# Moving the V projection's PSUM evictions from VectorE to ScalarE in an eight-core latent-attention layer

## The reference

```python
q_c = hidden_size @ Wq_c.T + bq_c
q = (q_c @ Wq_up.T + bq_up).reshape(b, s, NH, Q_HEAD).transpose(0, 2, 1, 3)
kv = hidden_size @ Wkv_c.T + bkv_c
kv_nope, kv_rope = (kv[..., :KV_LORA], kv[..., KV_LORA:])
kvu = (kv_nope @ Wkv_up.T + bkv_up).reshape(b, s, NH, QK_NOPE + V_HEAD).transpose(0, 2, 1, 3)
k_nope, v = (kvu[..., :QK_NOPE], kvu[..., QK_NOPE:])
k = jnp.concatenate([k_nope, broadcast(kv_rope)], axis=-1)
attn = softmax(q @ k.T / np.sqrt(Q_HEAD))
out = einsum('bhsv,Hv->bsH', attn @ v, Wo) + bo
```

## Time and profile before

| | us |
|---|---|
| two timed runs | 8833.02, 9584.68 (median 9208.85) |
| the profiled execution | 8920.18, span of its slowest core (core 1) 8918.6 |
| shortest span of a core in it | 8794.0 (core 6) |

### The profile page before, as it was taken

How to read it: one execution, slowest core, us unless ns; L and a number is a source line. 1 busy time by engine, 2 the same in 40 slices (tenths; PEclk the granted TensorE clock), 3 DMA queues, 4 the chain that set the end, 5 groups by cost and what they waited for, 6 DMA issues and landing times.

```text
span 8918.6 us, 102703 instructions; the slowest of 8 cores (8794.0 to 8918.6 us)
## 1 busy us (share of the span) xinstructions
PE 6759.7 (76%) x29896; PEld 2578.0 (29%) x29896; DVE 3238.8 (36%) x5966; ACT 3435.4 (39%) x5611; POOL 90.2 (1%) x168
## 2 busy tenths in 40 slices
PE   3555554555458898899889889889889889854878
PEld 1222222222223323323323322332332332312333
DVE  1112222222225534544543553553553553534111
ACT  2112333333314455355346346337337336442000
POOL 0000000000000000000000000000000000000000
PEclk9777676676679999999999999999999999966777
DMA  5552121111130000000000000000000000023343
GB/s 114 111 100 85 62 79 66 68 69 72 72 89 11 23 15 9 23 15 9 23 15 9 23 16 7 23 16 7 23 23 5 19 23 8 1 81 113 80 109 85
DMA packets 84513, 400.50 MB, mean 45 GB/s; under 512 B 7843, under 2 KB 20260, under 8 KB 65316
## 3 DMA queue, kind: packets, MB, share of 16 engines
q1 hardware_dynamic: 56678, 274.91, 8.6%
q0 software_dynamic: 27328, 119.02, 7.5%
HBM read 466.78 MB, written 46.14 MB: 58 GB/s over the span
## 4 chain that ended last, share of the span: by engine, by line
PE 68%; DVE 13%; issue 9%; DMA 8%; ACT 1%; another core or an unknown queue 1%; DVEq 0%; SPq 0%; ACTq 0%; POOL 0%; POOLq 0%
PE ps L692 8%; PE ps L316 7%; PE ps L656 7%; PE ps L978 6%; PE ps L650 6%; PE ps L706 6%; PE ps L695 5%; PE ps L653 5%; PE ps L370 5%; PE ps L573 4%; PE ps L538 3%; DVE arena L613 3%; DMA arena<-wqcT 2%; DVE arena L272 2%; DMA arena<-x_rot 2%
## 5 line engine op out<-in xcount | busy, mean ns | idle before, releaser
L667 ACT ACTIVATE arena<-ps,sb_negc_col 128x512 bf16<-128x512 f32 x2048 | 1407.9, 687 | 2542.5 <-DVE sb_negc_col L639 1647.1
L678 DVE TENSOR_TENSOR arena<-arena 128x512 bf16<-128x512 bf16 x2048 | 867.1, 424 | 2439.1 <-ACT arena L667 2282.8
L669 ACT ACTIVATE arena<-ps,sb_negc_col 128x512 bf16<-128x512 f32 x2048 | 1394.2, 681 | 0.0
L370 PE MATMUL ps<-sb_id,arena 128*128 128x128 f32 x2048 | 611.8, 348 | 984.8 <-DVE arena L272 955.4
L316 PE MATMUL ps<-arena 128*128 128x512 bf16 (+1 forms) x2560 | 813.3, 425 | 51.2 <-issue 51.2
L692 PE MATMUL ps<-arena 128*128 128x512 bf16 x2048 | 811.5, 396 | 38.7 <-DVE arena L743 38.0
L650 PE MATMUL ps<-arena 128*128 128x512 bf16 x2048 | 807.5, 394 | 31.5 <-ACT arena L669 31.5
L660 PE MATMUL ps<-arena 64*128 64x512 bf16 x2048 | 811.3, 396 | 0.0
L656 PE MATMUL ps<-arena 64*128 64x512 bf16 x2048 | 811.1, 396 | 0.0
L653 PE MATMUL ps<-arena 128*128 128x512 bf16 x2048 | 799.0, 390 | 0.0
L695 PE MATMUL ps<-arena 128*128 128x512 bf16 x2048 | 789.7, 386 | 0.0
(11 more groups left out here) (91 smaller groups left out, 4981.1 us busy)
## 6 DMA issues: line engine op xcount, KB each, us to landing
arena<-x_rot SPq DMA_DIRECT2D x72, 2048.0 KB, 7.8
arena<-wqcT POOLq DMA_DIRECT2D x64, 768.0 KB, 8.2
arena<-qcF_dram SPq DMA_DIRECT2D x32, 1536.0 KB, 6.3
arena<-wffn_til POOLq DMA_DIRECT2D x16, 2048.0 KB, 22.4
arena<-wqup_til POOLq DMA_DIRECT2D x16, 1152.0 KB, 9.0
x_dram<-arena SPq DMA_DIRECT2D x8, 2048.0 KB, 7.7
arena<-x_dram SPq DMA_DIRECT2D x8, 2048.0 KB, 28.5
out_c<-arena SPq DMA_DIRECT2D x64, 256.0 KB, 2.4
```

The costliest lines, as they stand in the source:

```text
L370: tok_tp = em("t", lambda t, b=b, xb=a_xn[bj], dc=dc: t.transpose(bank(b)[:, 0:128], xb[:, dc * 128:dc * 128 + 128], sb_id[:, :]), sm_t)
L667: te0 = em("s", lambda s, b0=b0, kc=kc: s.activation(b_P[0][kc % 3], bank(b0), AF.Exp, bias=sb_negc_col[:, :]), sm_s)
L669: te1 = em("s", lambda s, b1=b1, kc=kc: s.activation(b_P[1][kc % 3], bank(b1), AF.Exp, bias=sb_negc_col[:, :]), sm_s)
```

## The change

The 64 evictions of V of each pair, and the wait for the buffer `b_V` to be free in front of them, go from VectorE's list to ScalarE's. Their tokens come from ScalarE's semaphore. The instruction is a copy from PSUM (fp32) to SBUF (bf16) of the same 128x256 as before. TensorE's list is the same, but for the semaphore that it waits for.

```diff
@@ -596,7 +596,7 @@
             tkm = em("v", lambda v: v.tensor_reduce(
                 sb_kmax[:, :], sb_stab[:, 3:6], AX.X, ALU.max), sm_v)
             wt("t", tok_wv)
-            wt("v", tok_V_free)
+            wt("s", tok_V_free)
             tok_V_ready = None
             for tk in range(64):
                 b = prod_bank()
@@ -609,9 +609,9 @@
                         b_wkV[:, lat, :],
                         start=(lat == 0), stop=(lat == 3)),
                         sm_t if lat == 3 else None)
-                wt("v", tok_mm)
-                tok_V_ready = em("v", lambda v, b=b, tk=tk: v.tensor_copy(
-                    b_V[:, tk * 256:tk * 256 + 256], bank(b)[:, 0:256]), sm_v)
+                wt("s", tok_mm)
+                tok_V_ready = em("s", lambda e, b=b, tk=tk: e.copy(
+                    b_V[:, tk * 256:tk * 256 + 256], bank(b)[:, 0:256]), sm_s)
                 bankfree[b] = tok_V_ready
```

## The result

| | kernel before | changed kernel |
|---|---|---|
| median of the timed executions | 9498.35 us (10, from 8830.79 to 9659.61) | 9025.08 us (11, from 8500.07 to 9300.69) |
| ratio by comparable executions | | 0.967, 95% interval 0.958 to 0.976 |
| profiled execution, slowest core's span | 8918.6 us | 8498.5 us |

The changed kernel is faster, by the 3.3% of the ratio. In most timed executions of either kernel the four cores of one die, or all eight, have a lower mean granted clock and a longer span (in one of the changed kernel's, 0.766 to 0.771 and 9203 to 9299 us on cores 4 to 7, against 0.867 to 0.869 and 8464 to 8493 us on cores 0 to 3), which is why the two medians lie some 578 and 525 us above the profiled executions and the median of 9025 lies outside the predicted range of 8475 to 8660.

The account below looks back on a forecast made before the run. TensorE was taken to be bound by waits for V copies behind VectorE's reductions. Removing 331 us gave 8589 us from the profiled 8920 or 8502 from 8833; 8550 was put between, range 8475 to 8660.

Parts of the forecast that it names:

- The stall: V projection: TensorE waits for V copies standing behind two K reductions in VectorE's list; 17.49 us a pair removed.
- The slow clock behind it: V tiles after the wait: about 6.5 ran at 0.85 in place of 0.43 us; 2.7 us a pair removed.
- the sum: V stages of all pairs: 20.7 us a pair x 16 pairs = 331 us gained.
- The copy on ScalarE: V evictions: 406 ns each, a start every 0.30 us, under TensorE's 0.427, so costed at nothing.
- The cover: Behind K: VectorE's reductions and bound stay hidden under the V stage, with 7 us to spare.
- The wait did not move: Rival: TensorE waits at L635 for the bound instead of at L606; 219 us gain left, 8614 to 8701; chance 0.03.
- The tables: Rival: ScalarE reloads the exponential's table each pair, 1.28 us x 16 = 20 us at worst; chance 0.04.
- the rival of the throttled dies: Phase B: more even TensorE use brings a 0.81 clock, some 900 us added, 9490 us in all; chance 0.04.

Follow-up runs that it names:

- The short reductions: Kernel before with both maxima over K taken over 128 of 8192 columns, V copies left on VectorE: span 8534.8 us.
- the doubled reductions: Changed kernel with each of the two K reductions made twice in VectorE's list: span 8621.4 us.
- the run that was timed again: Changed kernel, unaltered, timed in turns with the kernel before on one chip: ratio 0.961, medians 8885.1 against 9153.4 us.

## Why the prediction was right in its steps and wrong in its time

**The stall.** Removed as said: 279.8 us of wait gone, no wait in its place. The short reductions show that its cause was the work in front of the copies in VectorE's list, and the wait follows their length.

**The slow clock behind it.** There as said, and mis-sized: priced at 2.7 us a pair, measured 27.2 / 16 = 1.7 (1.5 by the 240 matmuls behind the wait in a usual pair). The stage that I took for all had 48.5 us, the median stage 47.2: its stretch of half clock was the longest of the 16. And 64 tiles took 28.1 us, not 27.5. In the whole, 20.7 us a pair were reckoned; the V stages give 307 / 16 = 19.2, the pair distances 20.3. From the first V matmul of the loop to the last the two profiles differ by 323 us, of which 16 lie outside the V stages, where the sum had nothing. That the 331 us of the sum are also the 331 between the shortest timed executions is in part luck: a term that was too large was made up by one that was left out.

**The copy on ScalarE.** Reckoned at 406 ns and a start every 0.30; measured 373 and 0.263. Costed at nothing, and it cost nothing.

**The cover.** VectorE's chain has 8.1 us to spare before V's end, 7 were reckoned; the doubled reductions show it. The wait did not move.

**The tables.** One load in the phase, as before.

**What failed: the base from which the sum was taken.** The prediction said of the median of the two runs, 9208.85, "the middle of two unlike executions, and I don't reckon from it". It took the shorter of them and the profiled one as the only bases. The 9584.68 us was left out, and so was the question how often such an execution occurs. The runs showed it to be common: the median of the kernel before over 10 executions is 9498, of the changed one over 11 it is 9025. How common differs from one set of timings to the next: in three others, on three chips, the same kernel before had medians of 9287.76 (7 executions), 8844.08 (7) and 9153.41 us (11). The mechanism had been named, with its price, as the rival of the throttled dies, but as something that the change might bring on (0.04), and not as something that was there before it. The two runs in hand already said it: 9584.68 - 8833.02 = 752 us, not far from the 900 of the rival. From these two bases alone the time could lie anywhere from 8833 - 331 = 8502 to 9585 - 331 = 9254 us, and the range had to reach that far; the median is inside it. Within comparable executions the range held: 8500, and 3.3% where 3.7 was forecast.

**The throttled dies.** The Trainium skill's page "TensorE: Matmul & The Clock Gate" (section "Seeing it yourself") says that a die's clock goes to 13/16 when three of its cores run dense matmuls. By the prediction the trace disagreed in the attention. It does so in the profiled executions of both kernels; in the run that was timed again two cores of a die took up the lower grant in the middle of phase B, when all its cores had been at the same work for 3,000 us. And they were two: cores 0 and 1 fell to a mean of 0.90 there, cores 2 and 3 of the same die stayed at 0.96; these had theirs before, in phase A and in the first pair (318.5 us to the next on core 2, 304.2 on core 0). In the FFN of the kernel before it was also cores 0 and 1 that had 0.81; core 2 had 1.00 from 8700 to 8750 us, with TensorE busy throughout. So the rule tells of a grant that does occur, but here neither always nor on the whole die at once. Whether the change makes it more or less frequent, by TensorE's more even use, the executions here are too few to tell.

Left open: why cores take up the lower grant in one execution and not in another, which of them, and at which point. No run here varies its cause.

## What to carry to other kernels

A long instruction that nobody waits for can still be the stall, by what stands behind it in its engine's list: here the V copies behind two reductions. Ask of an idle engine whether it can take over what stands behind, and check that its own price back to back is under the producer's pace (0.263 against 0.43 us), as reordering alone leaves the sum of the engine's work as the bound (39 us against 28). Read more than one turn of a loop before pricing it: the one stage that was read here was the longest of 16. And before a time is forecast from a profile, ask how often an execution is like it: a median is of all of them.

## What the runs showed of the hardware

- A wait of 17.5 us in front of the same matmuls cost 1.5 us of half clock behind it in the usual pair, one of 4.7 us cost 2.7; some fifteen waits of 0.54 us in a row, 2.45 us apart, left the granted clock at 1.00.
- ScalarE copies from PSUM of 128x256 take 373 ns each and start 0.263 us apart when back to back; VectorE's take 424 ns and start 0.33 us apart.
- The lower grant can set in in the middle of an execution and on two cores of a die alone: pairs of 307.3 us became pairs of 321 to 326 us on core 0 and stayed 307 on core 2 of the same die and on core 4 of the other, after more than 3,000 us of the same loop.
